# Moving the second attention of a gated cross-attention stack from the expert passes into the MLP's first hidden layer, and the next MLP input's transposes ahead of w3

## What is computed

```python
x = x + tanh(g_xattn[0]) * two_way_gated_attention(layernorm(x), ctx)    # stage A
x = x + tanh(g_ffn[0]) * top_2_of_8_experts(layernorm(x))                # stage B
xp, yp = relu(layernorm(x) @ W.T + b), relu(ctx @ W.T + b)               # stage C
x = x + tanh(g_xattn[1]) * softmax(xp @ yp.T, masked) @ ctx
h = silu(xn @ w1.T * s1) * (xn @ w2.T * s2)       # xn = layernorm(x),     stage D
h = gelu(h @ h1.T * s3); h = gelu(h @ h2.T * s4)
x = x + tanh(g_ffn[1]) * (h @ w3.T * s5)
```

## Time and profile before

| | us |
|---|---|
| median of 3 runs | 1147.28 (1146.55 to 1148.4) |
| profiled execution | 1146.65 |
| its span, first to last instruction | 1144.9 |
| TensorE busy | 1091.8 (95%) |
| VectorE busy | 536.5 (47%) |
| ScalarE busy | 439.0 (38%) |

### The profile page before, as it was taken

The page is one execution under the profiler, slowest core; times in us unless marked ns, Lnnn a source line. Parts: engine busy times, 40 slices in busy tenths (PEclk is TensorE's granted clock), DMA queues, the critical chain, the costliest instruction groups (busy, mean ns, idle before and its releaser), DMA issues.

```text
span 1144.9 us, 15058 instructions
## 1 busy us (share of the span) xinstructions
PE 1091.8 (95%) x5194; PEld 866.2 (76%) x5194; DVE 536.5 (47%) x1437; ACT 439.0 (38%) x825; POOL 119.8 (10%) x164
## 2 busy tenths in 40 slices
PE   7989989899998999899999999999999999999997
PEld 4757767677666776588888888788788888888886
DVE  6567666876676766531421521512512412412411
ACT  1344441124224252643443443533533533533532
POOL 0015552200000000300100100100000000001001
PEclk9989989999999999899999999999999999999999
DMA  9200000610000100200000000000000000000000
GB/s 349 89 1 1 1 1 1 274 58 0 19 18 1 37 0 19 128 1 1 20 1 1 19 0 0 18 0 0 18 0 0 18 0 0 18 0 0 19 1 20
DMA packets 5320, 33.01 MB, mean 29 GB/s; under 512 B 1182, under 2 KB 1438, under 8 KB 3224
## 3 DMA queue, kind: packets, MB, share of 16 engines
q1 hardware_dynamic: 4584, 29.41, 6.5%
q10 hardware_dynamic: 688, 3.01, 0.7%
HBM read 28.23 MB, written 4.19 MB: 28 GB/s over the span
## 4 chain that ended last, share of the span: by engine, by line
PE 85%; DVE 7%; ACT 3%; issue 2%; POOL 1%; DMA 1%; DVEq 0%; SPq 0%; POOLq 0%; ACTq 0%
PE psum L839 55%; PE psum L735 12%; PE psum L754 2%; PE psum L470 2%; DVE x_residual L1537 1%; PE psum L557 1%; PE psum L533 1%; PE psum L762 1%; PE psum L571 1%; PE psum L715 1%; PE psum L782 1%; DMA x_residual<-in_x 1%; PE psum L587 1%; DVE ln_stats L1231 1%; DVE x_normalised L1242 1%
## 5 line engine op out<-in xcount | busy, mean ns | idle before, releaser
L839 PE MATMUL psum<-hidden_a_high,mlp_rest_rounded 128*128 128x512 f32 x512 | 199.8, 390 | 0.0
L839 PE MATMUL psum<-hidden_a_low,mlp_rest_rounded 128*128 128x512 f32 x512 | 199.3, 389 | 0.0
L839 PE MATMUL psum<-hidden_b_high,mlp_h_rounded 128*128 128x512 f32 x512 | 199.2, 389 | 0.0
L839 PE MATMUL psum<-hidden_b_low,mlp_h_rounded 128*128 128x512 f32 x512 | 199.2, 389 | 0.0
L1651 DVE TENSOR_TENSOR hidden_a_low<-hidden_a,hidden_a_high 128x512 fp32r<-128x512 f32 x128 | 88.5, 691 | 195.4 <-ACT hidden_a_high L1170 194.5
L1537 DVE SCALAR_TENSOR_TENSOR x_residual<-psum,expert_weight,x_residual 128x256 f32<-128x256 f32 (+1 forms) x256 | 108.5, 477 | 57.8 <-PE psum L735 56.9
L1651 DVE TENSOR_TENSOR hidden_b_low<-hidden_b,hidden_b_high 128x512 fp32r<-128x512 f32 x64 | 44.3, 692 | 179.9 <-ACT hidden_b_high L1170 178.5
L735 PE MATMUL psum<-expert_high,x_T_high 128*128 128x512 f32 x256 | 112.4, 439 | 4.6 <-DVE x_residual L1537 4.3
L839 PEld LDWEIGHTS psum<-hidden_a_high,mlp_rest_rounded 128*128 128x128 f32 x512 | 96.1, 188 | 21.5 <-DVE hidden_a_low L1651 1.5
L839 PEld LDWEIGHTS psum<-hidden_b_high,mlp_h_rounded 128*128 128x128 f32 x512 | 96.1, 188 | 20.0
L839 PEld LDWEIGHTS psum<-hidden_b_low,mlp_h_rounded 128*128 128x128 f32 x512 | 96.1, 188 | 19.9
(11 more groups left out here) (213 smaller groups left out, 1608.3 us busy)
## 6 DMA issues: line engine op xcount, KB each, us to landing
x_residual<-in_x SPq DMA_DIRECT2D x4, 1024.0 KB, 22.9
mlp_h_slice<-in_h SPq DMA_DIRECT2D x4, 1024.0 KB, 4.7
mlp_rest<-in_h SPq DMA_DIRECT2D x1, 4096.0 KB, 19.8
mlp_h<-in_h SPq DMA_DIRECT2D x1, 4096.0 KB, 12.4
out<-x_residual SPq DMA_DIRECT2D x8, 512.0 KB, 2.6
mlp_rest<-in_w SPq DMA_DIRECT2D x3, 1024.0 KB, 8.8
expert_in<-in_Wi SPq DMA_DIRECT2D x1, 2048.0 KB, 15.9
expert_out<-in_Wo SPq DMA_DIRECT2D x1, 2048.0 KB, 20.4
```

The costliest lines, as they stand in the source:

```text
L839: last = mm(o, a, b, start=(k == 0 and i == 0), stop=(k == n_k - 1 and i == len(parts) - 1))
```

## The change

The attention leaves the passes. A pass (`b_pass`) has the expert steps, the turn and the routing of the next group only; the last one (`b_last_pass`) has the attention of group 0 in it. The attention of group n+1 stands in MLP group n: its transposes, projection, scores and exponentials behind blocks 1 to 6 of h1, its product with the context behind block 0 of h2, its update and statistics on VectorE behind blocks 0 and 1 of h2. `c_turn` and `turn` transpose tiles in pairs, four transposes into one bank, and ScalarE and VectorE then copy a pair at once. `turn(n + 1)` stands on TensorE ahead of all of w3. On VectorE `norm(n + 1)` stays behind the loop over the layers; it waits for a new semaphore in place of the end of h2, and `low_turn` moves ahead of the updates. VectorE's loop over passes holds passes 1 to 6, and the MLP loops have two groups in their body, 1 to 6 in three rounds. At the entry of the MLP VectorE does `b_end` between `norm(0)` and `low_turn(0)`. The attention's weight W1T gets a DMA of its own, its tiles other places in SBUF; ScalarE's examination of the MLP weights is spread over the passes, written out without a loop. POOL inverts the statistics of group n+1 ahead of the additions of group n.

```diff
+            def transpose_pair(src, pair, done):
+                for k in range(KC):
+                    for i in range(2):
+                        last = pe.transpose(ps[:, pair, (2 * k + i) * P:(2 * k + i + 1) * P],
+                                            src[:, 2 * pair + i, k * P:(k + 1) * P], ident[:])
+                last.then_inc(done, 1)
+            def c_turn(c):
+                for pair in range(2):
+                    pe.wait_ge(xnc_r, 2 * pair + 2 + G * c)
+                    transpose_pair(xnc, pair, tpc)
...
+            def b_last_pass(g, s):
+                for i in range(G * E // 2):
+                    b_experts(g, s, i)
+                    if i == 3:
+                        pe.wait_ge(lg_r, NG)
+                        c_turn(0)
+                    if i == 5:
+                        c_project(0)
+                    if i == 6:
+                        c_scores_T(0, 0)
+                    if i == 7:
+                        c_scores(0)
+                    if i == 9:
+                        c_probs_T(0)
+                    if i == 11:
+                        c_attend(0, 0)
+                    if i == 14:
+                        check_weights()
...
                 def turn(n):
-                    for j in range(G):
-                        pe.wait_ge(xn_r, 2 * NT + 1 + j + G * n)
-                        pe.wait_ge(xT_r, 2 * NT - 1 + j + G * n)
-                        transposes(xd[:, j, :], j % 2, tp)
+                    for pair in range(2):
+                        pe.wait_ge(xn_r, 2 * NT + 2 * pair + 2 + G * n)
+                        transpose_pair(xd, pair, tp)
...
+                                if layer and c == HC - 1 and k == 1:
+                                    last.then_inc(xd_free, 1)
                             last.then_inc(d2_ps, 1)
-                    if first:
-                        pe.wait_ge(xupc, 1 + NT)
+                            if b is None:
+                                continue
+                            if layer == 0 and c == 1:
+                                c_turn(n + 1)
...
+                group(0, 0)
+                with pe.Fori(0, NG // 2 - 1) as i:
+                    group(2 * i + 1, i + 1)
+                    group(2 * i + 2, i + 1)
+                group(NG - 1, None)
...
+                            if b is None or layer:
+                                continue
+                            if c == 1:
+                                c_turn(n + 1)
...
+            def b_pass(g, s, first=False):
+                b_norm(g + 1, 1 - s, (0, 1))
+                if not first:
+                    b_end(g - 1)
+                b_norm(g + 1, 1 - s, (2, 3))
                 for m in range(G * E // 4):
-                    if c is None:
+                    if first:
                     b_add(g, s, m)
-                    for step in steps[m]:
-                        step()
-            dve.memset(PT[64:LP], 0.0).then_inc(zero_ready, 1)
-            dve.wait_ge(zero_ready, 8)
+                    if m == 0:
+                        b_low(g + 1, 1 - s, (0, 1))
+                    if m == 2:
+                        b_low(g + 1, 1 - s, (2, 3))
+                    if m == 3:
+                        b_measure(g, 0)
+                    if m == 5:
+                        b_route(g + 1, 1 - s)
+            def b_last_pass(g, s):
+                c_batch(0)
+                c_norm(0)
+                b_end(g - 1)
+                for m in range(G * E // 4):
+                    b_add(g, s, m)
+                    if m == 2:
+                        check_weights()
+                    if m == 3:
+                        c_max(0)
+                        b_measure(g, 0)
+                    if m == 5:
+                        c_update(0)
+                        c_stats(0)
             b_route(0, 0)
-            bc_pass(0, 0, None, None, True, None)
+            b_pass(0, 0, True)
             dve.wait_ge(inv, INV_A)
-            bc_pass(1, 1, 0, 0, True, None)
-            bc_pass(2, 0, 1, None, True, 0)
-            with dve.Fori(1, NG // 2 - 1) as i:
-                st.enter(i - 1, BC_STEPS)
-                bc_pass(2 * i + 1, 1, 2 * i, i, True, 2 * i - 1)
-                bc_pass(2 * i + 2, 0, 2 * i + 1, None, True, 2 * i)
-            st.leave(NG // 2 - 2)
-            bc_pass(NG - 1, 1, NG - 2, B - 1, False, NG - 3)
+            with dve.Fori(0, NG // 2 - 1) as i:
+                st.enter(i, B_STEPS)
+                b_pass(2 * i + 1, 1)
+                b_pass(2 * i + 2, 0)
+            st.leave(NG // 2 - 1)
+            b_last_pass(NG - 1, 1)
...
+                def group(n, b, fetch):
+                    if fetch:
+                        c_batch(b)
...
+                    if b is not None:
+                        c_norm(n + 1)
                     for layer, (full, part, rest) in enumerate(((hb_f, hb_h, hb_l), (ha_f, ha_h, ha_l))):
                         for c in range(HC):
                             low(c, full, part, rest, 3 * HC * n + HC * (layer + 1) + c + 1)
-                    if ahead:
-                        dve.wait_ge(d2_ps, 2 * HC * n + 2 * HC)
+                            if b is None:
+                                continue
+                            if layer == 0 and c == 4:
+                                c_max(n + 1)
+                            if layer == 1 and c == 0:
+                                c_update(n + 1)
+                            if layer == 1 and c == 1:
+                                c_stats(n + 1)
+                    if b is not None:
+                        dve.wait_ge(inv_c, n + 2)
+                        dve.wait_ge(xd_free, n + 1)
                         norm(n + 1)
+                    if b is not None:
+                        low_turn(n + 1)
                     update(n, 0)
                     update(n, 1)
-                    if ahead:
-                        low_turn(n + 1)
                     update(n, 2)
                     update(n, 3)
                 low_turn(0)
-                b_end(NG - 1)
-                dve.wait_ge(tp, 2 * NT + G)
-                c_norm(NG - 1)
-                c_stats(NG - 2)
-                group(0, True, first=True)
-                with dve.Fori(1, NG - 1) as n:
-                    group(n, True)
-                group(NG - 1, False)
+                group(0, 0, False)
+                with dve.Fori(0, NG // 2 - 1) as i:
+                    st.enter(i, D_STEPS)
+                    group(2 * i + 1, i + 1, True)
+                    group(2 * i + 2, i + 1, False)
+                st.leave(NG // 2 - 1)
+                group(NG - 1, None, False)
 
             dve.wait_ge(inv_c, 1)
-            dve.wait_ge(tpc, NT - G)
-            steps_before = st.n
+            norm(0)
+            b_end(NG - 1)
...
+            with pool.Fori(0, NG - 1) as n:
+                st.enter(n, 1)
+                invert(G * n + G, G, n + 2, stats_c, inv_c)
+                add(n)
+            st.leave(NG - 1)
+            add(NG - 1)
```

More of the change, by code:

```diff
@@ L658, in _ @@
             pe.wait_ge(map_v, 4)
[L659 removed]
+            project(w1t, 0)
             a_probs_back_T(0)
@@ L698, in _, with b_turn @@
             pe.wait_ge(ub_r, NT - JT)
-            def b_turn(g, s, tiles, before):
-                if before is not None:
-                    pe.wait_ge(xupc, 1 + G * before)
+            def b_turn(g, s, tiles):
                 for j in tiles:
@@ L723, in b_route @@
                 pe.wait_ge(rt_s, g + 1)
+                if before is not None:
+                    pe.wait_ge(lg_r, before + 1)
                 for j in range(G):
@@ L808, in bc_pass @@
                 for i in range(G * E // 2):
                     b_experts(g, s, i)
-                    if c is None and i % 2 == 0:
+                    if before is None and i % 2 == 0:
                         a_sum(B - 1, i // 2)
-                    for step in steps.get(i, ()):
-                        step()
-            b_turn(0, 0, range(G), None)
+                    if i == 2:
+                        b_turn(g + 1, 1 - s, (0, 1))
+                    if i == 4:
+                        b_turn(g + 1, 1 - s, (2, 3))
@@ L873, in group @@
                         last.then_inc(d1_ps, 1)
-                        if first and c in chain:
-                            chain[c]()
-                    if first:
-                        pe.wait_ge(h_r, HC)
                     for layer, (name, src) in enumerate((("h1", ha), ("h2", hb))):
@@ L1170, in high, with group @@
                         act.activation(part[:, c, :], full[:, c, :], ACT.Copy).then_inc(hi_r, 1)
[L1172 to L1175 removed]
+                def group(n, b):
                     for c in range(HC):
                         act.wait_ge(d1_ps, HC * n + c + 1)
[L1178 removed]
+                        act.activation(ha_f[:, c, :], ps[:, d_bank(c), :], ACT.Silu,
```

(8 more changed lines are left out.)

317 lines of the change are left out of this document (141 added, 176 removed).

## The result

| | before | after |
|---|---|---|
| median, runs side by side | 1147.84 (1146.55 to 1148.4) | 1167.03 (1165.59 to 1169.4) |
| ratio to before, 95% interval | | 1.0174 (1.0161 to 1.0188) |
| profiled execution | 1146.65 | 1167.56 |
| its span | 1144.9 | 1165.7 |
| TensorE busy | 1091.8 | 1100.6 |

The change costs 19.2 us by the medians and 20.8 by the two spans. The forecast was 1171.5 us, 24 slower, in a range of 1156 to 1181.

What follows compares the result with a forecast made beforehand. The prediction took TensorE to bound both touched stages, so only its idle time and clock could change. Its terms summed to +24.5 us on 1147.3, giving 1171.8, written as 1171.5 us, range 1156 to 1181.

Steps and rivals of the forecast that it cites:

- attention transposes: TensorE's waits for copies of the attention's transposes go, as c_turn fills two banks with pairs: -2.7 us.
- VectorE's pass loop: VectorE's loop over passes jumps back twice instead of once, each jump priced at 4.3 us: +4.0, bounds -4.6 to +4.6.
- entry: At the MLP's entry VectorE does b_end ahead of the two subtractions that complete the input: +0.7 us, bounds 0 and 2.
- attention out of group 0: The last group's attention leaves MLP group 0, with its waits of 1.3 and 0.8 us: -2.1 us.
- exponentials in h1: In h1, the probabilities' transposes wait 0.25 us for ScalarE's exponentials, seven times: +1.8 us, bounds 0 and 9.
- gap ahead of w3: TensorE idles 2.84 us after h2 for normalised tiles, seven groups, less waits that go: +10.9 us, range 9 to 12.
- falls behind it: TensorE's clock falls to 1.2 GHz behind each of seven gaps, 1.7 us each: +11.9 us, bounds 0 and 21.
- Rival (C): Normalisation ends before h2 does, so transposes ahead of w3 need not wait: about 1129 us, chance 0.05.
- (A): Rival: the clock holds through the seven gaps ahead of w3; sum +12.6, 1160 us; 1151 to 1164 given chance 0.17.
- The sign: Whole kernel slower by over 2.3 us: chance 0.92; within that 0.03, faster 0.05.

Runs made afterwards that it cites:

- e6: The kernel before with VectorE's loop over passes 3 to 6 written out; 1140.94 us, ratio 0.9943.
- e10: e8 with, at the MLP entry, normalisation of group 0 ahead of the last expert sum and b_end later, and the probabilities' transposes behind h1 block 7; 1123.22 us.
- e8: The changed kernel with the edits of e1, e4 and e5 together; 1127.98 us, ratio 0.9822.
- e4: The changed kernel with the routing's transposes and products one step later in each pass on TensorE; 1160.19 us, ratio 1.0123.
- e5: The changed kernel with MLP groups 1 to 6 written out on TensorE, ScalarE and VectorE instead of looped; 1164.03 us, ratio 1.0152.
- e1: The changed kernel with VectorE's normalisation of group n+1 behind block 6 of the last h2 layer instead of block 7; 1136.25 us, ratio 0.991.
- e7: The changed kernel with 120 satisfied waits added to each round of VectorE's pass loop, body 386 instructions instead of 266; 1191.23 us, ratio 1.0377.
- e11: The changed kernel with 60 satisfied waits added to each round of VectorE's pass loop, body 326 instructions; 1167.18 us, ratio 1.0166.
- e2: The changed kernel with the next MLP input's transposes back behind the second w3 tile, their low half between updates 1 and 2; 1140.24 us, ratio 0.995.
- e9: The changed kernel with four unused extra products on TensorE ahead of the wait for the normalised tiles, seven times; 1165.12 us, ratio 1.0143.
- e3: The changed kernel with eleven unused extra products on TensorE ahead of the wait for the normalised tiles, seven times; 1163.44 us, ratio 1.0142.

## Why the prediction was right, and where it was not

| term | forecast | measured | where it is read |
|---|---|---|---|
| attention transposes | -2.7 | -2.7 | wait gone |
| VectorE's pass loop | +4.0 | -4.6 to -5.9 | against 267.43; e6 |
| entry | +0.7 | +0.6 | 5.9 us from the last expert to w1, 5.3 before |
| attention out of group 0 | -2.1 | -2.1 | waits gone |
| exponentials in h1 | +1.8 | +1.8 to +2.6 | seven times 0.26 to 0.37; e10 against e8 |
| gap ahead of w3 | +10.9 | +10.6 | 19.8 of waits less 9.2 that went |
| falls behind it | +11.9 | +8 | six at 1.2 to 1.5 |
| routing on x_T_low | 0 | +4.2 to +5.4 | six waits; e4 |
| jumps of the MLP loop | 0 | +3.1 | e5 |
| w1 and w2 of group 0, first pass, stage A | 0 | +2.7 | see below |

The gap was right step by step: the last low half, four normalisations, two tiles before the first transpose, 2.84 us forecast (its links add up to 2.82) and 2.81 measured. It and the falls are nearly all of the loss, and e1, which removes just them, turns it into a gain. Rival (C) had named that point: with the normalisation done before h2 ends, 1129. The changed kernel did not do it, so (C) was rightly set low; e1 did and gave 1136, and e8, with the waits of the routing and of the MLP's jumps gone as well, 1128.

**The step that failed** is the pass loop. I had priced a jump from the one in the trace and multiplied by two, although I had written that the body becomes shorter and that this could do away with the stall. The forecast put the term at +4.0; -4.6 to -5.9 was measured. The runs show that the length of the body decides: 326 instructions go through, 386 from the same place do not, and the 350 of the kernel before did not. The Trainium skill (Runtime: NRT & Kernel Launch, Instruction fetch mechanics) has the rule, a stall only where the branch's target has left the engine's instruction store, and the runs fit it: the shorter bodies jump at once. The figure of 512 instructions that the Trainium skill gives there for that store is no length that is safe, since a body of 350 stood still for 2.51 us: the measurement decides. The same question, asked of the other loop that the change made longer, TensorE's MLP loop with two groups in its body, would have led to the two waits of 1.4 and 1.6 us. I looked at the jump that was in the trace and not at the one that the diff made.

**The term that was mis-sized** is the falls: 1.7 us each, taken from stretches at half clock, against 1.2 to 1.5 from group to group, and one of seven did not come. (The prediction's line that no wait of the MLP before is over 0.81 us leaves out group 0, where the 1.3 us on the exponentials stood.) (A) is answered as well: through gaps of 2.8 us the clock mostly does not hold. The Trainium skill (TensorE: Matmul & The Clock Gate, Why this matters for your kernels) tolerates gaps of that size; 27 falls behind 35 of them in five kernels (the changed one, e4, e5, e7, e11) speak against it.

**The terms that were missing** are those of work whose cover left. I asked for each moved step what it would wait for in its new place, and not what it had covered in the old one. The routing lost its cover in six passes. The +2.7 of the last row are small: four waits of w1 and w2 in group 0 on hidden_a (1.0 us in all), 0.6 and 0.3 us more at the start of pass 1, and 0.8 us up to there, where executions of the same code differ by more than that; none of the three was tried apart.

The measured column adds up to 20 to 24 us, against 20.8 of the spans. What was missing (+10) and what was put too high (-13) nearly cancel, so that the time came out within 5 us was luck. The sign was not: the gap with its falls, 18.6 us, outweighs the 9.4 to 10.7 us that the change gains. The gap alone would about balance them.

## What to carry to other kernels

When work is moved to the front of a stage, look for what its input stands behind on the other engine, and whether by data or only by order: here one block earlier in VectorE's list was worth 30 us. For each step that leaves a place, ask what it covered there, and move what comes next. Where a loop's body changes length, look at its jump on every engine, in the timeline behind it.

## What the runs showed of the hardware that I had not expected

- The clock falls behind a gap in some groups and not in others of the same run: behind 27 of 35 gaps of 2.81 to 2.91 us, 4 of 7 of 1.91 us, none of 7 of 0.33. Those are gaps ahead of eight transposes, and transposes without a gap (e1) brought no fall. The transposes are not needed for it: four of six gaps of 2.34 to 2.37 us ahead of the routing's products brought one (e7). At the jumps of the MLP loop, gaps of 1.39 to 1.96 us with dense products behind them brought none in 14 (changed kernel, e1, e2, e4, e7, e9, e11) and one in two in e3, right behind a gap of 1.93 us. Whether what follows makes the difference at that length stays open.
- VectorE went through the jump of its loop at once with bodies of 266 and 326 instructions and stood still for 2.5 to 2.9 us with 350 and 386. It cost TensorE more than that (5.4 us in e6), by the late sums and a fall of the clock.
- On TensorE a body of two MLP groups (856 products and transposes, each with its weight load) waited 1.4 to 2.0 us at each jump; the body of one group (392), in the kernel before, showed no such wait.
- Satisfied waits are not free on VectorE: 60 calls, 30 instructions, held it up for some 2.3 us (e7).
